# A one-core chain of eight transformer layers: first keys by pieces, router weights split early, two weight buffers exchanged, 24 products of ones in front

## The reference

```python
x = x + tanh(g_xattn[0]) * L0_xattn(layernorm(x), ctx, ctx, Wq, Wk, Wv, Wo)   # 32 heads of 16, 8 key/value heads
x = x + tanh(g_ffn[0])   * L0_ffn(layernorm(x), ...)    # dense 512x512 + 8 LoRA experts, top 2 of a softmax router
x = x + tanh(g_xattn[1]) * L1_xattn(layernorm(x), ctx, ...)   # RMSNorm inside, else shaped as L0
x = x + tanh(g_ffn[1])   * L1_ffn(layernorm(x), ...)    # int8-quantized gated MLP
... # L2 and L3: attentions with heads of 128, a fake-quantized linear layer, a router of 4 experts

# inside an attention
q = (query @ Wq) ; k = (key @ Wk) ; v = (value @ Wv)    # query = layernorm(x), key = value = ctx
out = softmax(q @ k^T * scale) @ v ; return out @ Wo
```

## Time and profile before

| | us |
|---|---|
| three runs | 1656.87, 1658.82, 1658.66 |
| the profiled execution, its own time | 1655.67 |
| its span, first to last instruction | 1653.8 |
| TensorE busy | 1534.1 (93% of the span) |
| VectorE / ScalarE / GpSimd busy | 901.5 / 699.4 / 636.6 |
| mean granted TensorE clock | 0.982 of full |

### The profile page before, as it was taken

One profiled execution on the slowest core, in us unless ns is written; L12 is line 12 of the kernel. 1 busy time (PEld: TensorE's weight loads), 2 busy tenths in 40 slices (PEclk: granted clock), 3 DMA queues, 4 the chain that ended last, 5 costly groups with the idle time before them and its releaser, 6 DMA issues.

```text
span 1653.8 us, 25537 instructions
## 1 busy us (share of the span) xinstructions
PE 1534.1 (93%) x8786; PEld 1217.7 (74%) x8786; DVE 901.5 (55%) x1805; ACT 699.4 (42%) x2005; POOL 636.6 (38%) x606
## 2 busy tenths in 40 slices
PE   5897989888699999999999999889899999999998
PEld 4565766567578888888888887667677777777776
DVE  5786668858621222222231124688766776776666
ACT  4443154435335444453544444543344333443442
POOL 3544145557423221331323132334644544444430
PEclk9998999999989999999999999999999999999998
DMA  5001001021211010100101011114312212112101
GB/s 211 26 1 51 20 26 39 1 99 45 53 50 52 14 52 1 65 26 28 36 17 52 1 52 50 40 44 111 107 52 64 77 52 71 59 58 71 30 14 52
DMA packets 27885, 81.41 MB, mean 49 GB/s; under 512 B 3248, under 2 KB 11952, under 8 KB 22768
## 3 DMA queue, kind: packets, MB, share of 16 engines
q1 hardware_dynamic: 26896, 79.44, 14.5%
q10 hardware_dynamic: 864, 0.30, 0.1%
HBM read 69.25 MB, written 10.49 MB: 48 GB/s over the span
## 4 chain that ended last, share of the span: by engine, by line
PE 52%; issue 12%; DVE 5%; POOL 3%; ACT 1%; POOLq 0%; DVEq 0%; ACTq 0%
PE bank L397 32%; PE bank L1342 7%; PE bank L1330 2%; PE pair L2404 2%; PE bank L2382 2%; PE pair L1311 2%; POOL wo_low L388 1%; PE bank L1319 1%; PE pair L397 1%; POOL wq_low L1067 1%; PE bank L2390 1%; POOL probs L1076 1%; DVE small L222 0%; DVE probs L2236 0%; DVE out_low L2266 0%
## 5 line engine op out<-in xcount | busy, mean ns | idle before, releaser
L397 PE MATMUL bank<-hid_high,wq_high 128*128 128x512 f32 (+1 forms) x640 | 255.0, 398 | 2.4 <-issue 2.2
L1252 DVE SCALAR_TENSOR_TENSOR x_stream<-bank,gates,x_stream 128x512 f32<-128x512 f32 x64 | 48.0, 751 | 351.6 <-PE bank L1342 351.6
L397 PE MATMUL bank<-hid_high,wq_low 128*128 128x512 f32 (+1 forms) x640 | 238.0, 372 | 0.0
L397 PE MATMUL bank<-hid_low,wq_high 128*128 128x512 f32 (+1 forms) x640 | 236.4, 369 | 0.0
L1076 POOL TENSOR_TENSOR probs<-probs,small 128x512 f32<-128x512 f32 x64 | 67.2, 1050 | 356.7 <-DVE small L1240 356.7
L2131 ACT ACTIVATE probs<-probs,small 128x64 f32<-128x64 f32 x256 | 86.1, 338 | 135.2 <-DVE small L2255 135.2
L397 PEld LDWEIGHTS bank<-hid_high,wq_high 128*128 128x128 f32 x640 | 120.9, 189 | 25.9 <-issue 5.0
L397 PEld LDWEIGHTS bank<-hid_high,wq_low 128*128 128x128 f32 x640 | 120.8, 189 | 22.7
L397 PEld LDWEIGHTS bank<-hid_low,wq_high 128*128 128x128 f32 x640 | 121.3, 190 | 20.5 <-issue 3.4
L1150 ACT ACTIVATE probs<-pair,small 128x128 f32<-128x128 f32 x256 | 90.7, 367 | 82.6 <-DVE small L1234 80.2
L599 POOL TENSOR_TENSOR probs<-probs,small 128x512 f32<-128x512 f32 x64 | 67.2, 1051 | 122.5 <-DVE small L801 122.3
(11 more groups left out here) (351 smaller groups left out, 3985.5 us busy)
## 6 DMA issues: line engine op xcount, KB each, us to landing
raw_q<-in_L_wq SPq DMA_DIRECT2D x18, 1024.0 KB, 5.0
raw_o<-in_L_wo SPq DMA_DIRECT2D x18, 1024.0 KB, 4.9
values<-ctx_values SPq DMA_DIRECT2D x32, 256.0 KB, 3.9
values_t<-ctx_keys SPq DMA_DIRECT2D x8, 512.0 KB, 3.3
raw_c<-in_L_wkv SPq DMA_DIRECT2D x6, 512.0 KB, 3.4
raw_o<-in_L_wkv SPq DMA_DIRECT2D x5, 512.0 KB, 4.8
x_stream<-in_x SPq DMA_DIRECT2D x8, 256.0 KB, 9.7
ctx_keys<-raw_o SPq DMA_DIRECT2D x8, 256.0 KB, 2.0
```

The costliest lines, as they stand in the source:

```text
L397: last = k.nc.tensor.matmul(out, stationary(a, c), moving(b, c), start=n == 0, stop=n == total - 1)
L1252: nc.vector.scalar_tensor_tensor(xt, k.bank[7][:], gate, xt, ALU.mult, ALU.add).then_inc(k.x_done, 1)
```

## The change

1. **Order of loads.** The key/value weights are issued behind context piece 0 rather than piece 1, and the query weights behind x tile 3 rather than tile 7.
2. **Keys by pieces.** ScalarE casts the key/value weights between context pieces 0 and 1; TensorE multiplies each context piece for both key banks as its low part appears, instead of waiting for all.
3. **Values in other banks and later.** In L0 the values go to banks 0 and 1, one ahead of transpose 0 and one ahead of transpose 2.
4. **L0's lists.** ScalarE casts the query weights ahead of the key copies and alternates value copies, casts of transposed tiles and query copies. GpSimd alternates powers and query-weight reductions. VectorE's statistics go tile pair by tile pair with normalising and low parts between.
5. **Router weights** are cast at n = 8 and reduced at n = 10 and 11.
6. **Two buffers exchanged.** L1's query weights and F1's gate/up weights use `wo`; L1's output weights and F1's down weights use `wq`. So L1's query weights can be split right behind L1's key/value weights, and value copies stand between the first scalings of L1's normalised tiles.
7. **Warm-up.** TensorE starts with 24 float32 products of a 128x128 tile of ones into bank 7.

```diff
 def prologue(k, block):
@@ sync
             sp.dma_start(RAW[c], ...).then_inc(k.loaded_ctx[c], 16)
-            if c == 1:
+            if c == 0:
                 fetch_ahead(k, sp, "L0", "c")
         for t in range(T):
             sp.dma_start(k.x[:, t * D:(t + 1) * D], ...).then_inc(k.loaded_x[t], 16)
-        fetch_ahead(k, sp, "L0", "q")
+            if t == 3:
+                fetch_ahead(k, sp, "L0", "q")
         fetch_ahead(k, sp, "L0", "o")
@@ scalar
             nc.scalar.copy(hv[:, c, :, 0, :], ...).then_inc(k.xt_hi, 1)
+            if c == 0:
+                act.wait_ge(k.loaded_c, 16)
+                split_high_scalar(k, act, k.raw_c, k.wc, 1024, k.hi_c)
+    @block.tensor
+    def _(pe):
+        pe.wait_ge(k.pool_step, 1)
+        for _ in range(WARM_UP):                      # WARM_UP = 24
+            nc.tensor.matmul(k.bank[7][:, 0:P], k.ones[:], k.ones[:], start=True, stop=True)
+QUERY_PARTS = ((0,), (1, 2), (3,), ())
 def attention16(k, layer, rms, block):
+    WQ, WO = (k.wo, k.wq) if rms else (k.wq, k.wo)
+    VALUE_BANK = 4 if rms else 0
@@ gpsimd
         if rms:
+            split_low_gpsimd(k, pool, k.raw_q, WQ, 2048, k.hi_q, k.at("hi_q", 0), k.lo_q)
...
-        split_low_gpsimd(k, pool, k.raw_q, k.wq, 2048, k.hi_q, k.at("hi_q", 0), k.lo_q)
+        else:
+            for p in range(T // 2):
+                ln_rstd_gpsimd(k, pool, p, p + 1 - k.early)
+                for c in QUERY_PARTS[p]:
+                    cols = slice(512 * c, 512 * c + 512)
+                    pool.wait_ge(k.hi_q, k.at("hi_q", c + 1))
+                    nc.gpsimd.tensor_tensor(WQ[1][:, cols], k.raw_q[:, cols], WQ[0][:, cols],
+                                            ALU.subtract).then_inc(k.lo_q, 1)
...
-                if n in (24, 25):
-                    dense_low_c(n - 24)
+                if n in (10, 11):
+                    dense_low_c(n - 10)
@@ scalar
+        if rms:
+            act.wait_ge(k.loaded_c, k.at("loaded_c", 16))
+            split_high_scalar(k, act, k.raw_c, k.wc, 1024, k.hi_c)
+            act.wait_ge(k.y_psum, k.at("y_psum", 0))
+        high_q()
         for h in range(2):
             act.wait_ge(k.kv_psum, k.at("kv_psum", h + 1))
             nc.scalar.copy(k.kt[:, 512 * h:512 * h + 512], k.bank[4 + h][:]).then_inc(k.kv_sbuf, 1)
...
+            for h in range(2):
+                value_copies(h)
+                for t in (2 * h, 2 * h + 1):
+                    ln_high_scalar(k, act, t)
+            for h in range(2):
+                queries(0, h)
+                for t in (2 * h + 4, 2 * h + 5):
+                    ln_high_scalar(k, act, t)
...
-                if n == 23:
+                if n == 8:
                     high_c()
@@ vector
+            for p in range(T // 2 + 2):
+                if p < T // 2:
+                    for t in (2 * p, 2 * p + 1):
+                        dve.wait_ge(k.loaded_x[t], 16)
+                        ln_tile_vector(k, dve, t)
+                    ln_variance_vector(k, dve, p, p + 1 - k.early)
+                if 1 <= p <= T // 2:
+                    for t in (2 * p - 2, 2 * p - 1):
+                        ln_apply_vector(k, dve, t)
+                if p >= 2:
+                    for t in (2 * p - 4, 2 * p - 3):
+                        ln_low_vector(k, dve, t)
@@ tensor
+        def keys_by_chunk():
+            pe.wait_ge(k.lo_c, k.at("lo_c", 1))
+            for c in range(C):
+                pe.wait_ge(k.xt_lo, k.at("xt_lo", c + 1 - C))
+                for h in range(2):
+                    for s, m in PAIRS:
+                        last = nc.tensor.matmul(k.bank[4 + h][:], k.wc[s][:, c * P:(c + 1) * P], hid_cols(...), ...)
...
+            if not rms and t in (0, 2):
+                context(1, t // 2, k.bank[t // 2])
             ln_transpose_tensor(k, pe, t, k.xs_ready if rms else k.xn_ready)
 def quant_mlp(k, block):
-                split_low_gpsimd(k, pool, k.raw_o, k.wo, 1024, k.hi_o, k.at("hi_o", 0), k.lo_o)
+                split_low_gpsimd(k, pool, k.raw_o, k.wq, 1024, k.hi_o, k.at("hi_o", 0), k.lo_o)
```

104 lines of the change are left out of this document (53 added, 51 removed).

## The result

The changed kernel takes **1640.08 us** (median of 4 runs, 1636.75 to 1641.37) against 1658.01 of the kernel before (4 runs on the same chip): ratio 0.989, 95% interval 0.9874 to 0.9905, 17.9 us less: a small gain, but the whole interval lies below 1. The forecast was 1640.4.

The account below looks back on a forecast made before the run. TensorE, busy for most of the span, was taken as the bound, so gains are its waits or slow running. 8.4 + 7.7 + 2.2 = 18.3 us off 1658.66 gave 1640.4; 8 of 10 within 1633 to 1647.

Parts of the forecast that it names:

- Start of L0, 8.4 forecast: Earlier query weights and new order move VectorE's first score maximum from 43.23 to 33.8; 8.4 us after deduction, bounds 4 to 10.5.
- the term that I took off for the collision of VectorE and GpSimd: Start of L0: GpSimd's four subtractions beside VectorE's normalising cost 1.0 us, bounds 0 to 8.6.
- the 2 us on either side: Whole kernel: allowance around 1636 to 1646 us for low-clock stretches that fall elsewhere.
- The products of ones: priced at 0: Start of L0: 24 warm-up products cost nothing, covered by ScalarE's query-weight work; about 3 us if slow throughout.
- The collision as a rival: Start of L0: VectorE and GpSimd collide in full, 4.3 us instead of 1.0, giving 1643.7; chance 0.07.
- The rule that I drew in the prediction: VectorE and GpSimd's shared port is an exclusive lock, so every overlap costs the loser a full instruction.
- Router, 7.7: L0's router product: early weight split removes a 5.8 us wait and the slow stretch behind; 7.7 us, bounds 5.8 to 8.9.
- L1, 2.2: L1's start: scalings ahead of value copies bring the first transposed tile's cast 1.8 earlier; 2.2 us, bounds 1.5 to 2.8.
- F1, 0: F1: the same products out of other buffers, 0 us.
- the 18.3: Whole kernel: total gain in us, 8.4 at L0's start, 7.7 at the router and 2.2 in L1.
- bounds of 13 to 23: Whole kernel: the terms' bounds taken together, in us gained, giving 1636 to 1646 us.
- rival by falls of the clock (slower): L0 onward, loops too: small gaps drop TensorE to 1.2 GHz again and again, seven stretches more, giving 1662; chance 0.02.

Follow-up runs that it names:

- l1_old_order: The changed kernel with L1's start back in the old order, the two buffers still exchanged; median 1643.32 us.
- router_late: The changed kernel with the router weights' split back at its old place (cast in step 23, reduced in 24 and 25); median 1647.75 us.
- second profile of the changed kernel: From a second set of runs of the changed kernel, unaltered; median 1639.49 us, ratio 0.9887 to the kernel before.
- fill: The changed kernel with products of ones also in TensorE's waits at the starts of L0 (8) and L1 (8 and 3); median 1638.28 us.
- before_again: The kernel before, run and profiled a second time unaltered; median 1658.63 us over 11 runs, ratio 0.9999.
- fill_loop: As fill, with products of ones also in larger later waits of L0 (step 34) and L1 (steps 5, 6, 27, 28, 31); median 1634.73 us.
- no_warm_up: The changed kernel without the 24 products of ones at the start; median 1639.28 us.
- fill_all: As fill_loop, with products of ones at thirteen more places, in stages the change does not touch; median 1634.46 us.

## Why the prediction was right

*Start of L0, 8.4 forecast.* Measured 7.83 in one profile and 9.30 in the other, on either side (7.3 and 8.8 against the second profile of before). The chain was the one described, landing, four casts, four subtractions, two halves of queries, but not alone: the third transposes, through ScalarE and VectorE, end within 0.5 us of it. Landing came at 17.46 for 17.1, the low parts at 24.84 for 24.2. Where no fall disturbs it, the start gives 0.9 more than forecast (0.4 against the second profile of before). Part of that is the term that I took off for the collision of VectorE and GpSimd: 1.0, where it lengthens a pair by 1.9 but costs the chain 0.3 to 0.8, since the third transposes wait for ScalarE nearly as long; the rest is in the hand-overs and is not told apart. What takes it back in the first profile, a fall of the clock in the queries (1.1 to 1.5 us), I had put nowhere but in the 2 us on either side. The products of ones: priced at 0, measured 0.3 at most. No run takes out the keys by pieces, the values in other banks or the new order of VectorE's and GpSimd's lists; what each of them is worth within the start is not shown.

*The collision as a rival.* It is real and did not decide the time. VectorE's normalising (2.90 for 1.00) and the low part of a context piece (1.99 for 1.23) slowed beside GpSimd; the low parts read from a bank (1.27 for two) and the statistics (0.69) did not. The Trainium skill, "SBUF — State Buffer", section "SBUF: two separate sides", ties the lock to VectorE operations in a 2-port mode, or with two inputs from SBUF while GpSimd reads SBUF. The context piece has two such inputs, and the operations that were not slowed have one at most, so these rows agree with it; the mode of the normalising no row shows. The rule that I drew in the prediction, by which every overlap costs, was too wide.

*Router, 7.7.* Measured 7.93 and 7.92 in the two profiles (7.4 against the second of before), 7.45 and 7.7 by undoing it, 7.7 or 7.0 alone. Right with its two parts, the wait and the slow stretch behind it, and the new place costs 0.

*L1, 2.2.* The mechanism was right and its size too: counted from L0's last maximum, L1's first transposes come 1.90 earlier, and with equal falls the stretch gains 2.0. But in the changed kernel only 0.45 arrives against the first profile of before (15.87 to 16.32, 17.41 to 17.85), and against the second, whose stretch has no fall, it is 0.9 us longer than before. Both profiles of the changed kernel have two falls there, one of them in L1's first queries, where neither profile of before has one. Here a step of the prediction failed: it counted the wait and not the clock behind the waits that stayed (1.60 and 0.64). Why the fall comes there is open: it is not L1's order (l1_old_order has it), and not the waits alone (router_late has them without it).

*F1, 0.* Held within the 3 us by which one program's time behind L1 varies.

*The sum.* By L1's last maximum the changed kernel is 15.0 and 18.1 ahead of the first profile of before, 13.8 and 16.9 ahead of the second; the medians say 17.9 and 18.9, since both profiles of before ran under their medians, by 2.3 and 1.7. In the second profile of the changed kernel the 18.3 came out because L1's 1.75 too much stood against 0.9 too little at the start and 0.2 at the router. In the first the three terms give 16.2, and L1's loop loses 1.3 more. That the median lies 0.3 us from the forecast is therefore partly luck; the mechanisms of the start and of the router, 16.1 of the 18.3, are not. The forecast's bounds of 13 to 23 are also not the sum of its terms' bounds, which is 11.3 to 22.2. The rival by falls of the clock (slower) had the sign wrong, but its mechanism is there, once in L1 in both profiles and once more in L0's queries in one; over the first 350 us it took no more than before (12.0 and 6.7 us of clock against 10.3 and 8.4).

## What to carry to other kernels

When a wait of TensorE is removed, look at the waits that stay near it: the clock behind them, and not their length, may decide what of the gain arrives, and it may differ from one execution to the next. One profile of each kernel leaves 1.5 us at a milestone and 3 us at the end of a stage open, so take a second before explaining less than that, and compare stretches that hold the same number of falls. Products of ones in TensorE's waits won 5 us here, in waits for data. In the one wait tried that ends with the engine's own sequencer they could not start before its end, and pushed the work back by 3.0 us.

## What the hardware did that I had not expected

- Falls to the 1.2 GHz level came behind a single wait of 1.98 us (at 148.8 in fill), and behind pairs such as 0.75 and 1.23 at 229 and 231. The same wait of 1.98 stands without a fall in before_again (166.27) and router_late (157.43), so the wait alone does not settle it. Each fall took 1.7 us of clock; the three that fill had ahead of L1's last maximum and fill_loop had not (5.2 us of clock) gave 4.5 us of time. The Trainium skill, "TensorE: Matmul & The Clock Gate", section "A second HAM failure mode: psum-queue depth-cycling", tells of frequent small waits between groups of products that make the clock go up and down. The falls behind pairs agree with it; those behind the single wait of 1.98 are no such case.
- The granted clock in the profile's columns reads 1.00 over the slow products at the start of before and of no_warm_up (24 keys in 7.56 us): there only the spacing shows the level.
- More clock was not more speed: fill_all ran at 0.992 and took as long as fill_loop at 0.982.
